# Local attention in a hybrid block: two heads per score matmul, row sums over 128 partitions, queries on the partitions of the result

## The chip, the cores and the metric

The kernel runs on one core of a Trainium2 chip. The metric is the device time of one execution in microseconds. PE is the matmul engine (its weight loads are listed apart, as PEld), DVE the vector engine, ACT the scalar engine, POOL is GpSimd, SP the queue that issues transfers. [...]

## The reference

A windowed-attention block with an MLP, then a landmark attention and a mixture of experts. The change lies in the first of these, which is the only part quoted (x is 16 x 32 x 32 x 128, windows of 8 x 8 tokens, 16 heads of 8 channels):

```python
win = shifted.reshape(B, H_ // WS, WS, W_ // WS, WS, C).transpose(0, 1, 3, 2, 4, 5).reshape(-1, N, C)
qkv = (win @ qkv_w.T + qkv_bias).reshape(-1, N, 3, NH, hd).transpose(2, 0, 3, 1, 4)
attn = jnp.einsum('bhnd,bhmd->bhnm', _l2n(q), _l2n(k)) * scale
attn = attn + rpb[None]                        # relative position bias
attn = attn.reshape(-1, nW, NH, N, N) + ATTN_MASK[None, :, None]
attn = jax.nn.softmax(attn.reshape(-1, NH, N, N), axis=-1)
out = jnp.einsum('bhnm,bhmd->bhnd', attn, v).transpose(0, 2, 1, 3).reshape(-1, N, C)
out = out @ proj_w.T + proj_b
x = x + _ln(out, norm1_g, norm1_b)
```

## The kernel before

The program is a row of phases (setup, this attention, MLP, landmarks, an iterated inverse, mixing, experts) with a barrier between them. Only the attention phase and a few constants of the setup are touched.

The attention phase works on 128 pairs of windows (16 images, 8 pairs each; 128 tokens on 128 partitions). It is written out without loops: `beats` calls each engine's `beat(s)` for s from -5 on, and the order inside `beat` is that engine's order. A beat holds stages of several pairs. In beat s, PE does: `scores` of pair s+1 (L627, 16-bit, only for the row maxima), the projection of pair s-2 (L673, L674), transposes (of q and k, L682, in even beats; of x, L692, in odd ones), `turned_scores` of pair s (L640 brings in maxima and mask, L645 the 32-bit scores, keys on partitions), the transpose of the maxima of s+1 (L704), and `values` of pair s-1 (L662). In odd beats it ends with the q, k products (L716, L717) and the v product (L721) for the two pairs s+5 and s+6. In `values`, both the outputs (`vd`) and the row sums (`den`) are matmuls whose result has channels on partitions, four accumulated parts for each.

DVE does in a beat: reciprocal of the sums of s-2 (L545), normalized output `onT` (L548), row maxima of s+1 (L554), statistics and first half of the layer norm of s-2 (L561 to L566), a slice of the inverse norms of q and k, and the output row (L602). ACT in even beats: squares (L495), `qT` (L501), four masked copies `km` (L504, one head of every four each), exp of pair s (L516), the maxima `mT` of s+1 (L522). In odd beats: `xT` (L512), exp, `mT`, then `qk` (L527) and `vd` (L532) out of PSUM. POOL multiplies the exponentials by the exponential of the position bias (L483) between exp and `values`.

The wait before the transpose of the maxima matters below. Bank 5 of PSUM is shared by it, by the transposes of x and by the v product:

```python
                            if s.odd:
                                unit(pe, xT_ok, s + 5)
                            else:
                                unit(pe, v_ok, s + 4)
```

`met` and `unit` wait for the named signal of a pair or of a unit of two pairs. `apart` adds an instruction between two waits.

## Time and profile before

| what | us |
|---|---|
| median of 3 runs | 4109.78 |
| lowest, highest of them | 4073.84, 5130.18 |
| the profiled execution, its own time | 4067.03 |
| its span in the trace | 4065.2 |
| mean granted TensorE clock over the span | 0.809 |

The span is what the trace shows, and the profiled execution took 1.8 us more than it. All rows come from that one execution. A clock of 1.00 in a view is 2.4 GHz, 0.50 is 1.2 GHz, and a value between is a mean over a stretch that held both. "issue" as a releaser means that the engine waited for nothing that the profile shows.

### The profile page before, as it was taken

Reading aid. Unit: us, or ns where it says so; the run is one execution under the profiler, and the core shown is the slowest. Engines: PE = TensorE matmul, PEld = TensorE weight load, DVE = VectorE, ACT = ScalarE, POOL = GpSimd, SP = SyncE. Lnnn points to the kernel's source line nnn. Section 1 sums busy time; section 2 is a strip of 40 time slices with the busy share of each in tenths; the row PEclk is TensorE's granted clock in tenths of the full one; section 3 lists DMA queues with packets and bytes.
Section 4 is the critical chain, followed back from the end, with each engine's and each line's share of the span. In section 5 each row is a group of like instructions: output and inputs, shape, how many; then the busy total and the mean of one; then the engine's idle time right before and its main releaser. Section 6 shows DMA issues by size and latency. Waiting matters only on the chain. (4 is left out here: it accounts for less than half of the span.)

```text
span 4065.2 us, 136261 instructions
## 1 busy us (share of the span) xinstructions
PE 3284.9 (81%) x55527; PEld 2395.2 (59%) x55527; DVE 2493.4 (61%) x6382; ACT 1486.0 (37%) x2726; POOL 1295.9 (32%) x1363
## 2 busy tenths in 40 slices
PE   3787777777787897999988888888874999877777
PEld 2555555555555575777788665555653666555444
DVE  3555565555565455888777677666663777555555
ACT  1323332233232343333300333333322677545454
POOL 1333333333333232111000155555553000244444
PEclk9756665666666898999989888777776999988888
DMA  2000000000000121000000011111113444322222
GB/s 85 17 17 18 17 18 17 17 17 17 17 18 14 55 71 54 22 21 21 11 4 3 25 49 42 42 40 37 47 34 81 97 96 96 79 63 63 62 63 57
DMA packets 298547, 165.00 MB, mean 41 GB/s; under 512 B 98300, under 2 KB 289160, under 8 KB 297736
## 3 DMA queue, kind: packets, MB, share of 16 engines
q1 hardware_dynamic: 281608, 123.42, 11.3%
q0 software_dynamic: 16384, 33.59, 2.8%
q8 instruction: 420, 6.88, 0.7%
q14 instruction: 135, 1.11, 0.1%
HBM read 67.00 MB, written 71.30 MB: 34 GB/s over the span
## 5 line engine op out<-in xcount | busy, mean ns | idle before, releaser
L2251 DVE TENSOR_TENSOR e_glo<-e_g,e_ghi 128x512 f16<-128x512 f32 x540 | 373.4, 691 | 270.0 <-ACT e_ghi L2158 188.9
L2153 ACT ACTIVATE e_g<-psum,b 128x512 f32<-128x512 f32 x540 | 368.9, 687 | 387.1 <-PE psum L2307 255.6
L2324 PE MATMUL psum<-w2hi,e_ghi 128*128 (+1 forms) x2160 | 419.3, 227 | 99.8 <-DVE e_glo L2251 72.0
L2137 POOL DMA_INDIRECT e_got<-ys_dram,e_idx x256 | 257.8, 1007 | 698.7 <-DMA ys_dram<-e_yo 421.3
L2328 PE MATMUL psum<-w2hi,e_glo 128*128 (+1 forms) x2160 | 415.2, 227 | 10.0 <-issue 9.5
L2326 PE MATMUL psum<-w2lo,e_ghi 128*128 (+1 forms) x2160 | 415.2, 227 | 9.1 <-issue 7.9
L483 POOL TENSOR_TENSOR pT<-pT,rpbx 128x1024 f32<-128x1024 f32 x128 | 301.1, 2352 | 192.8 <-ACT pT L516 192.8
L2324 PEld LDWEIGHTS psum<-w2hi,e_ghi 128*128 128x128 f16 x2160 | 219.1, 101 | 234.6 <-DVE e_glo L2251 112.7
L545 DVE RECIPROCAL rd<-psum 128x128 f32<-128x128 f32 x128 | 122.5, 957 | 300.3 <-PE psum L662 297.6
L1687 POOL DMA_INDIRECT xs_dram<-m_xt,m_idxl x256 | 265.4, 1037 | 113.3 <-issue 72.6
L554 DVE TENSOR_REDUCE mx<-psum 128x16 f16<-128x1024 f32 x128 | 156.2, 1220 | 195.2 <-PE psum L627 194.8
L2326 PEld LDWEIGHTS psum<-w2lo,e_ghi 128*128 128x128 f16 x2160 | 219.6, 102 | 55.9 <-issue 21.6
L2158 ACT ACTIVATE e_ghi<-psum,b 128x512 f16<-128x512 f32 x334 | 227.8, 682 | 0.0
L2328 PEld LDWEIGHTS psum<-w2hi,e_glo 128*128 128x128 f16 x2160 | 220.3, 102 | 10.2 <-issue 9.6
L662 PE MATMUL psum<-pT,den 64*32 64x64 f32 x8192 | 164.4, 282 | 73.6 <-issue 73.6
L662 PE MATMUL psum<-pT,vd 64*32 64x64 f32 x8192 | 159.7, 292 | 78.0 <-issue 76.6
L472 POOL TENSOR_TENSOR rstd<-mv,eps 128x1 f32<-128x1 f32 x128 | 24.2, 189 | 602.7 <-DVE mv L564 602.7
L1973 PEld LDWEIGHTS psum<-m_zd,m_p1T 128*128 128x128 f32 x1024 | 147.6, 222 | 87.6 <-issue 59.7
L1973 PE MATMUL psum<-m_zd,m_p1T 128*128 128x34 f32 x1024 | 154.7, 301 | 40.0 <-issue 25.3
L645 PE MATMUL psum<-qT,km 32*64 32x64 f32 x8192 | 166.1, 304 | 24.0 <-issue 23.9
L662 PEld LDWEIGHTS psum<-pT,den 64*32 64x32 f32 x8192 | 130.3, 130 | 88.1 <-issue 88.1
L1922 PE MATMUL psum<-m_klm,m_qT 128*128 128x512 f32 x256 | 182.2, 804 | 0.0
(331 smaller groups left out, 8010.4 us busy)
## 6 DMA issues: line engine op xcount, KB each, us to landing
ys_dram<-e_yo SPq DMA_DIRECT2D x71, 256.0 KB
f_xm<-x_dram SPq DMA_DIRECT2D x32, 256.0 KB
mid_dram<-f_xm SPq DMA_DIRECT2D x32, 256.0 KB
l_t<-mid_dram SPq DMA_DIRECT2D x16, 512.0 KB
m_t<-mid_dram SPq DMA_DIRECT2D x16, 512.0 KB
res_dram<-m_rest SPq DMA_DIRECT2D x16, 512.0 KB
e_acc<-res_dram SPq DMA_DIRECT2D x32, 256.0 KB
out_dram<-e_acc SPq DMA_DIRECT2D x32, 256.0 KB
```

The lines of the kernel that those rows point to most:

```text
L483: gp.tensor_tensor(pT[:, s.odd], pT[:, s.odd], rpbx[:], ALU.mult).then_inc(pe_ok.sem, 1)
L662: i = pe.matmul(bank(6 + w)[rows(c), N * k:N * k + N], wt, pT[half(w), q.odd, 4 * c + h, :], start=(h == 0), stop=(h == 3), skip_group_che ...
L1687: gp.indirect_dma_start(out=xs, out_offset=bass.IndirectOffsetOnAxis(idxl[w.odd][:, k, t:t + 1], 0), in_=xt16[w.odd][:, t].rearrange("p h ...
L1922: pe.matmul(bank(2 + q.r), qT[q.odd][:, q.t * P:(q.t + 1) * P], klm[q.odd][:].rearrange("p h l -> p (h l)"), start=True, stop=True)\
L1973: i = pe.matmul(bank(6)[:, n * h:n * h + n], p1T[:, j.r, h, :], zd[j.odd][:, h].rearrange("p a d -> p (a d)"), start=True, stop=True)
L2137: gp.indirect_dma_start(out=got[:, q % 2, k, t, :], out_offset=None, in_=ys, in_offset=bass.IndirectOffsetOnAxis(idx[:, q // 2, i:i + 1], 0))\
L2153: ac.activation(g32[:, c % 4, :], bank(c % 4), ACT.Gelu, bias=bias, scale=1.0 / WSCALE)\
L2158: ac.activation(ghi[:, c % 4, :], bank(c % 4), ACT.Gelu, bias=bias, scale=1.0 / WSCALE)\
L2251: ve.tensor_tensor(glo[:, c % 4, :], g32[:, c % 4, :], ghi[:, c % 4, :], ALU.subtract)\
L2324: pe.matmul(o, ghi[:, c % 4, g], w2hi[:, e, f, :], start=first and t == 0, stop=False, skip_group_check=True)
L2326: pe.matmul(o, ghi[:, c % 4, g], w2lo[:, e, f, :], start=False, stop=False, skip_group_check=True)
L2328: i = pe.matmul(o, glo[:, c % 4, g], w2hi[:, e, f, :], start=False, stop=True, skip_group_check=True)
```

## The change

The scores are laid out anew. The masked operand is now q (`qm`, two heads side by side in 128 columns) and not k, so that `scores` has 16 matmuls of 128 result partitions (two heads by 64 queries), and `turned_scores` has 16 + 16 matmuls of 128 columns where there were 32 + 32 of 64. The exponentials of two heads then lie one above the other on 128 partitions. `values` becomes `sums`: 16 matmuls, whose stationary operand is a 128 x 64 block of exponentials and whose moving operand is `vd`, 18 columns wide and block-diagonal: 8 channels and a column of ones for the upper head, 8 and ones for the lower one. Row sums come with the outputs, and queries stand on partitions, so the reciprocal is of 16 numbers per partition (`rs`) and the result `on` must be transposed (a new PE step, a new copy `onT` by ACT) ahead of the projection.

`vd` must hold the tokens of a window twice, so `xT` is written twice over, and the v product runs once per pair (`value_rows`, in every beat) with the window's tokens doubled, copied out by two activations of 64 partitions. The x1 row and its store move one beat later, the layer norm to the end of DVE's beat, and squares on ACT from the even beat's start to the odd beat's end. The phase gets one more beat. In the setup, the bias table is written in two halves, and `den1` is gone.

```diff
...
-                vd = keep("vd", [P, 4, 8, 160])
-                den1 = keep("den1", [P, 4, 32])
...
+                vd = keep("vd", [P, 4, 4, NH // 2, 2, HD + 1])
...
+            qm = sb("qm", [P, 2, 2, 2, 2, 2, N])
             mT = sb("mT", [P, 2, P], F16)
-            pT = sb("pT", [P, 2, NH, N])
...
+            pT = sb("pT", [P, 2, 4, 2, 2 * N])
...
-                            gp.tensor_tensor(pT[:, s.odd], pT[:, s.odd], rpbx[:], ALU.mult).then_inc(pe_ok.sem, 1)
+                            p = pT[:, s.odd]
+                            e = rpbx[:].rearrange("p (j g) n -> p j (g n)", j=4).unsqueeze(2).to_broadcast([P, 4, 2, 2 * N])
+                            gp.tensor_tensor(p, p, e, ALU.mult).then_inc(pe_ok.sem, 1)
...
+                    def value_rows(q):
+                        if q.real():
+                            met(ac, v_ps, q)
+                            met(ac, o_ps, q - 8)
+                            for k in range(2):
+                                half = slice(64 * k, 64 * k + 64)
+                                src = bank(5)[half, 256:512].rearrange("p (w h k d) -> p w h k d", w=2, k=2, d=HD)
+                                i = ac.activation(vd[half, q.u, 2 * q.odd:2 * q.odd + 2, :, k, 0:HD], src[:, :, :, k, :], ACT.Copy)
+                            i.then_inc(v_ok.sem, 1)
+                    def masked(q, g):
+                        if q.real():
+                            ac.activation(qm[:, q.u % 2, :, g % 2, :, g // 2, :],
+                                          bank(4)[:, 0:2 * P].rearrange("p (a w t) -> p a w t", a=2, w=2), ACT.Copy, scale=msk[:, g:g + 1]).then_inc(qm_ok.sem, 1)
                     def beat(s):
                         if not s.odd:
...
                             q = s + 2
                             if q.real():
                                 unit(ac, tr_ps, q)
...
+                                ac.activation(kT[:, q.u % 2].rearrange("p a t -> p (a t)"), bank(4)[:, 2 * P:4 * P], ACT.Copy)\
+                                    .then_inc(kT_ok.sem, 1)
+                            masked(q, 0)
+                            masked(q, 1)
                         else:
                             q = s + 5
                             if q.real():
...
+                                met(ac, v_ps, q - 3)
+                                ac.activation(xT[:, q.u % 2], bank(5)[:, 0:2 * P].rearrange("p (a t) -> p a t", t=N).unsqueeze(2)
+                                              .to_broadcast([P, 4, 2, N]), ACT.Copy).then_inc(xT_ok.sem, 1)
+                        q = s - 2
+                        if q.real():
+                            met(ac, onT_ps, q)
+                            met(ac, pj_ps, q - 2)
+                            ac.activation(onT[:, q.odd, :], bank(6)[:, 0:P], ACT.Copy).then_inc(onT_ok.sem, 1)
+                        if not s.odd:
+                            masked(s + 2, 2)
+                            masked(s + 2, 3)
                         if s.real():
                             met(ac, t_ps, s)
...
+                            ac.activation(pT[:, s.odd].rearrange("p j w n -> p j (w n)"), turned, ACT.Exp).then_inc(pr_ok.sem, 1)
+                        if not s.odd:
+                            value_rows(s + 5)
                         q = s + 1
                         if q.real():
                             met(ac, mT_ps, q)
...
                             ac.activation(mT[:, q.odd, :], bank(5)[:, 0:64].bitcast(F16), ACT.Copy).then_inc(mT_ok.sem, 1)
                         q = s + 5
-                        if s.odd and q.real():
...
-                            unit(ac, v_ps, q)
...
+                        if s.odd:
+                            if q.real():
...
+                            value_rows(q)
+                            if q.real():
...
-                            ve.reciprocal(rd[:], outs[:, :, N:2 * N]).then_inc(rd_ok.sem, 1)
...
+                            ve.reciprocal(rs[:], heads_out[:, :, HD]).then_inc(rs_ok.sem, 1)
+                            met(ve, rs_ok, q)
+                            met(ve, onT_ps, q - 2)
+                            ve.tensor_tensor(on[:, q.odd, :].rearrange("p (h d) -> p h d", d=HD), heads_out[:, :, 0:HD],
+                                             rs[:].unsqueeze(2).to_broadcast([P, NH, HD]), ALU.mult).then_inc(on_ok.sem, 1)
                         q = s + 1
                         if q.real():
                             met(ve, s_ps, q)
                             met(ve, mT_ps, q - 2)
                             ve.tensor_reduce(mx2[:, q.kind(), :].rearrange("p (j r) -> p j r", j=4)[:, :, 0:4],
...
+                        unit(pe, kT_ok, q)
+                        unit(pe, qm_ok, q, 4)
                         met(pe, pr_ok, q - 2)
                         met(pe, mx_ok, q - 1)
-                        apart(pe)
...
+                        for w in range(2):
+                            for k in range(2):
                                 for j in range(4):
...
-                                                  high(qT[rows(j), q.u % 2, q.odd, half(w)]),
...
+                                    i = pe.matmul(bank(j)[:, 64 * (2 * w + k):64 * (2 * w + k) + 64],
+                                                  high(qm[rows(j), q.u % 2, q.odd, k, w].rearrange("p g t -> p (g t)")),
+                                                  high(kT[rows(j), q.u % 2, q.odd, half(w)]), start=True, stop=True)
                         i.then_inc(s_ps.sem, 1)
                     def turned_scores(q):
                         met(pe, mx_ok, q + 1)
                         met(pe, mT_ok, q)
-                        apart(pe)
...
+                        for w in range(2):
+                            for k in range(2):
+                                for j in range(4):
+                                    pe.matmul(bank(j)[half(k), 256 + P * w:256 + P * w + P], selk[rows(j), q.kind(), 2 * w + k, :],
+                                              mT[rows(j), q.odd, :], start=(w == 0), stop=False, skip_group_check=True)
+                        for w in range(2):
+                            for k in range(2):
+                                for j in range(4):
+                                    i = pe.matmul(bank(j)[half(k), 256 + P * w:256 + P * w + P],
+                                                  kT[rows(j), q.u % 2, q.odd, half(w)],
+                                                  qm[rows(j), q.u % 2, q.odd, k, w].rearrange("p g t -> p (g t)"),
+                                                  start=False, stop=(w == 1), skip_group_check=True)
+                        i.then_inc(t_ps.sem, 1)
+                    def sums(q):
+                        met(pe, pe_ok, q)
+                        met(pe, v_ok, q)
+                        met(pe, on_ok, q - 1)
+                        for j in range(4):
+                            for g in range(2):
+                                for w in range(2):
+                                    h = 2 * j + g
+                                    i = pe.matmul(bank(7)[half(w), 2 * (HD + 1) * h:2 * (HD + 1) * (h + 1)],
+                                                  pT[:, q.odd, j, w, N * g:N * g + N],
+                                                  vd[:, q.u, 2 * q.odd + w, h].rearrange("p k d -> p (k d)"), start=True, stop=True)
+                        i.then_inc(o_ps.sem, 1)
+                    def value_rows(q):
+                        if q.real():
+                            unit(pe, xT_ok, q)
+                            met(pe, v_ok, q - 1)
                             for w in range(2):
...
-                    def values(q):
...
-                        apart(pe)
...
-                                        wt = vd[half(w), q.u, 4 * q.odd + c, 32 * h:32 * h + 32] if k == 0 else den1[half(w), h, :]
...
+                                i = pe.matmul(bank(5)[:, 256 + C * w:256 + C * w + C],
+                                              xT[:, q.u % 2, 2 * q.odd + w].rearrange("p r t -> p (r t)"), wqkT[:, 2 * C:3 * C],
+                                              start=True, stop=True)
+                            i.then_inc(v_ps.sem, 1)
...
                         q = s + 5
-                        if s.odd and q.real():
+                        if not s.odd:
+                            met(pe, mT_ok, s)
+                            value_rows(q)
+                        elif q.real():
...
+                            met(pe, v_ok, q - 1)
                             met(pe, mT_ok, s)
                             for a in range(2):
                                 i = pe.transpose(bank(5)[:, P * a:P * a + P], xw[:, q.p + a, :], ident[:])
                             i.then_inc(xT_ps.sem, 1)
+                        q = s - 2
+                        if q.real():
+                            met(pe, on_ok, q)
+                            met(pe, h_ok, q - 1)
+                            pe.transpose(bank(6)[:, 0:P], on[:, q.odd, :], ident[:]).then_inc(onT_ps.sem, 1)
                         if s.real():
                             turned_scores(s)
...
-                                unit(pe, v_ok, s + 4)
+                                met(pe, v_ok, s + 5)
                             pe.transpose(bank(5)[:, 0:64].bitcast(F16), mx2[:, q.kind(), :], ident16[:]).then_inc(mT_ps.sem, 1)
+                        q = s - 2
+                        if q.real():
+                            met(pe, onT_ok, q)
+                            pe.matmul(bank(6)[:, P:2 * P], onT[:, q.odd, :], projT[:], start=True, stop=False)
+                            pe.matmul(bank(6)[:, P:2 * P], ones16[0:64, :], pb2[:], start=False, stop=True)\
+                                .then_inc(pj_ps.sem, 1)
                         q = s - 1
                         if q.real():
-                            values(q)
+                            sums(q)
...
                             met(pe, mT_ok, s + 1)
...
+                            value_rows(q)
...
```

PE in an odd beat before, from `scores` to `values`, and in an odd beat now:

```order
L627 MATMUL psum<-km,qT 64x64 x32
L673 MATMUL psum<-projT,onT 128x128
L674 MATMUL psum<-pb,ones 128x128
L692 MATMUL psum<-ident,xw 128x128 x2
L640 MATMUL psum<-mT,selk 64x64 x32
L645 MATMUL psum<-qT,km 64x64 x32
L704 MATMUL psum<-ident,mx 128x128
L662 MATMUL psum<-pT,vd 32x64 x32
L662 MATMUL psum<-pT,den 32x64 x32
```

```order
L654 MATMUL psum<-kT,qm 128x64 x16
L724 MATMUL psum<-ident,xw 128x128 x2
L730 MATMUL psum<-ident,on 128x128
L666 MATMUL psum<-mT,selk 64x128 x16
L671 MATMUL psum<-qm,kT 64x128 x16
L741 MATMUL psum<-ident,mx 128x128
L745 MATMUL psum<-projT,onT 128x128
L746 MATMUL psum<-pb,ones 128x128
L686 MATMUL psum<-vd,pT 64x18 x16
```

The five groups of 32 become four groups of 16, the projection moves behind the transposed maxima, and the transpose of `on` (L730) is new. ACT in an even beat before, and now (`qm`, `vd`, `onT` as above):

```order
L495 ACTIVATE sq<-qk 128x512
L501 ACTIVATE qT<-psum 128x256
L504 ACTIVATE km<-psum,msk 128x2x128 x4
L516 ACTIVATE pT<-psum 128x1024
L522 ACTIVATE mT<-psum 128x128
```

```order
L519 ACTIVATE kT<-psum 128x256
L510 ACTIVATE qm<-psum,msk 128x2x2x64 x2
L534 ACTIVATE onT<-psum 128x128
L510 ACTIVATE qm<-psum,msk 128x2x2x64 x2
L541 ACTIVATE pT<-psum 128x1024
L504 ACTIVATE vd<-psum 64x16x8 x2
L548 ACTIVATE mT<-psum 128x128
```

The `vd` copies of pair s+5 now stand between exp and `mT`, and in even beats PE's transpose of the maxima (L741) waits for them.

## Rows read from the trace of the kernel before

**Rows 1.** The page: span, and granted clock in 40 equal slices, in tenths.

```profile
span 4065.2 us, 136261 instructions
...
PEclk9756665666666898999989888777776999988888
```

**Rows 2.** Attention phase: length, busy us of PE, PEld, DVE, ACT, POOL; clock, DMA.

```profile
75.00:1340.00 1265.00, 977.80 (x34304) 702.47 (x34302) 700.93 (x1536) 384.36 (x832) 449.41 (x511) 0.65 0.06 17
```

**Rows 3.** Row maxima (L554) by line: count, first and last start.

```profile
L554 DVE TENSOR_REDUCE mx<-psum x128: 1211/1223/1226, 89.4 to 1313.4; 128x16 f16<-128x1024 f32 x128
```

**Rows 4.** Idle of the weight loads by line and releaser: total us, times, longest.

```profile
PEld psum L662 <- issue: 169.6, 117, 2.5
...
PEld psum L673 <- DVE onT L548: 58.5, 50, 1.7
...
PEld psum L627 <- issue: 40.1, 88, 2.3
PEld psum L645 <- issue: 27.3, 19, 2.9
```

**Rows 5.** Weight loads in the setup, in order: start, length, idle before.

```profile
31.34 1.80 PEld L320 LDWEIGHTS psum<-cpw,relx 128*32 128x32 f32 x128 [1.93 <-issue]
```

**Rows 6.** Weight loads in two beats of the attention, in order.

```profile
1009.69 0.89 PEld L645 LDWEIGHTS psum<-qT,km 32*64 32x64 f32 x64
...
1010.81 0.68 PEld L662 LDWEIGHTS psum<-pT,vd 64*32 64x32 f32 x63
...
1014.41 0.16 PEld L662 LDWEIGHTS psum<-pT,den 64*32 64x32 f32 x9 [2.36 <-issue]
...
1023.99 0.40 PEld L662 LDWEIGHTS psum<-pT,den 64*32 64x32 f32 x19 [1.79 <-issue]
...
1027.50 0.93 PEld L721 LDWEIGHTS psum<-wqkT,xT 128*128 128x128 f32 x4 [0.22 <-issue]
...
1031.19 1.20 PEld L645 LDWEIGHTS psum<-qT,km 32*64 32x64 f32 x64
...
1032.72 0.93 PEld L662 LDWEIGHTS psum<-pT,vd 64*32 64x32 f32 x63
...
1035.26 0.51 PEld L662 LDWEIGHTS psum<-pT,den 64*32 64x32 f32 x42 [1.24 <-issue]
```

**Rows 7.** DMA by queue, 1000 to 1100 us.

```profile
q8 instruction: 21, 0.34, 1.6%
```

**Rows 8.** Granted clock in short stretches of the attention and of the inverse.

```profile
1007.20:1017.20 10.00, 6.24 (x305) 4.75 (x305) 8.23 (x13) 4.42 (x11) 3.50 (x4) 0.99 0.05 12
1020.00:1034.00 14.00, 12.45 (x378) 8.86 (x378) 5.73 (x14) 5.67 (x12) 3.56 (x5) 0.50 0.06 17
2087.80:2090.30 2.50, 2.25 (x71) 2.06 (x67) 1.48 (x5) 0.00 (x0) 1.02 (x4) 1.00 0.00 0
2094.30:2096.30 2.00, 1.93 (x36) 1.96 (x38) 1.35 (x4) 0.00 (x0) 0.00 (x0) 0.50 0.00 0
```

**Rows 9.** Weight loads of 64x64 in the iterated inverse, moving operand of 16 columns.

```profile
2088.83 1.36 PEld L1434 LDWEIGHTS psum<-p_ay,p_xs 64*64 64x64 f32 x43 [0.33 <-issue]
```

**Rows 10.** Weight loads of 64x64 there, at the lower clock.

```profile
2094.34 2.88 PEld L1434 LDWEIGHTS psum<-p_t,p_ay 64*64 64x64 f32 x52 [1.16 <-issue]
```

**Rows 11.** Weight loads of 128x128 in the landmark phase.

```profile
1650.91 1.86 PEld L1271 LDWEIGHTS psum<-l_v,l_p3T 128*128 128x128 f32 x16
```

**Rows 12.** Costliest groups by line, 100 to 1300 us.

```profile
L483 POOL TENSOR_TENSOR pT<-pT,rpbx 128x1024 f32<-128x1024 f32 x124 | 291.7, 2353 | 187.7 <-ACT pT L516 187.7
...
L516 ACT ACTIVATE pT<-psum 128x1024 f32<-128x1024 f32 x123 | 127.3, 1035 | 114.0 <-PE psum L645 114.0
...
L545 DVE RECIPROCAL rd<-psum 128x128 f32<-128x128 f32 x123 | 117.7, 957 | 286.1 <-PE psum L662 283.4 <-issue 2.5
...
L522 ACT ACTIVATE mT<-psum 128x128 f16<-128x128 f16 x123 | 35.6, 289 | 0.0
```

**Rows 13.** Who waited for whom, PE, 100 to 1300 us.

```profile
PE psum L640 <- DVE mx L554: 14.0, 37, 0.9
```

More of the change, by code:

```diff
@@ L243, in _ @@
                             n += 1
-                        for k in range(4):
+                        for k in range(2):
                             gp.wait_ge(s_po, n)
-                            gp.memset(den1[:, k, 8 * k:8 * k + 8], 1.0).then_inc(s_po, 1)
+                            gp.memset(vd[64 * k:64 * k + 64, :, :, :, k, HD:HD + 1].rearrange("p u a h d -> p (u a h) d"), 1.0)\
+                                .then_inc(s_po, 1)
                             n += 1
+                        gp.wait_ge(s_po, n)
                         gp.wait_ge(s_ac, 2)
@@ L266, in _ @@
                         ac.wait_ge(s_ac, 4)
-                        ac.activation(rpbx[:].rearrange("q h n -> q n h"), sig[:], ACT.Exp, scale=16.0).then_inc(s_ac, 1)
+                        for k in range(2):
+                            half = slice(64 * k, 64 * k + 64)
+                            ac.activation(rpbx[half].rearrange("q h n -> q n h"),
+                                          sig[half].rearrange("q n (h k) -> q n h k", k=2)[:, :, :, k], ACT.Exp, scale=16.0)\
+                                .then_inc(s_ac, 1)
                     @block.vector
@@ L431, in beats @@
             def beats(eng, body):
-                for s in range(-5, NP * NB + 3):
+                for s in range(-5, NP * NB + 4):
                     body(Pair(0, s))
@@ L452, in beat @@
                         load(s + 8)
-                        q = s - 2
+                        q = s - 3
                         if q.real():
@@ L515, in beat @@
                             met(ac, o_ps, s - 2)
-                            ac.activation(pT[:, s.odd].rearrange("p (j g) n -> p j (g n)", j=4), turned, ACT.Exp)\
-                                .then_inc(pr_ok.sem, 1)
+                            ac.activation(pT[:, s.odd].rearrange("p j w n -> p j (w n)"), turned, ACT.Exp).then_inc(pr_ok.sem, 1)
+                        if not s.odd:
+                            value_rows(s + 5)
                         q = s + 1
@@ L598, in beat @@
                             k = q.p % 4
-                            met(ve, h_ok, q)
-                            met(ve, rstd_ok, q)
-                            met(ve, xb_ok, q)
-                            ve.scalar_tensor_tensor(out=x1[:, q.p, :], in0=h1[:, q.odd, :], scalar=rstd[:, k:k + 1],
-                                                    in1=x1[:, q.p, :], op0=ALU.mult, op1=ALU.add).then_inc(x1_ok.sem, 1)
+                            y = bank(6)[:, P:2 * P]
+                            met(ve, pj_ps, q)
+                            ve.bn_stats(st[:, k, :], y).then_inc(st_ok.sem, 1)
+                            met(ve, st_ok, q)
+                            apart(ve)
+                            ve.bn_aggr(mv[:, k, :], st[:, k, :]).then_inc(mv_ok.sem, 1)
+                            met(ve, mv_ok, q)
+                            ve.scalar_tensor_tensor(out=h1[:, q.odd, :], in0=y, scalar=mv[:, k, 0:1], in1=g1[:],
+                                                    op0=ALU.subtract, op1=ALU.mult).then_inc(h_ok.sem, 1)
                     beats(ve, beat)
@@ L635, in turned_scores @@
                         met(pe, mT_ok, q)
-                        apart(pe)
-                        for g in range(4):
-                            for w in range(2):
-                                for j in range(4):
-                                    pe.matmul(bank(j)[half(w), 256 + 64 * g:320 + 64 * g], selk[rows(j), q.kind(), g, half(w)],
-                                              mT[rows(j), q.odd, half(w)], start=(g == 0), stop=False, skip_group_check=True)
-                        for g in range(4):
-                            for w in range(2):
-                                for j in range(4):
-                                    i = pe.matmul(bank(j)[half(w), 256 + 64 * g:320 + 64 * g],
-                                                  km[rows(j), q.u % 2, q.odd, g, half(w)], qT[rows(j), q.u % 2, q.odd, half(w)],
-                                                  start=False, stop=(g == 3), skip_group_check=True)
@@ new lines, in turned_scores @@
+                        for w in range(2):
+                            for k in range(2):
+                                for j in range(4):
[3 more added lines that the diff above has]
+                                                  start=False, stop=(w == 1), skip_group_check=True)
@@ L719, in beat @@
                             met(pe, mT_ok, s + 1)
-                            for a in range(2):
-                                i = pe.matmul(bank(5)[:, 2 * P + C * a:2 * P + C * a + C], xT[:, q.u % 2, P * a:P * a + P],
-                                              wqkT[:, 2 * C:3 * C], start=True, stop=True)
-                            i.then_inc(v_ps.sem, 1)
+                            value_rows(q)
                     beats(pe, beat)
```

133 lines of the change are left out of this document (43 added, 90 removed).

## The prediction

> **What bounds the kernel now.** I read the slices of the page first, then the attention phase alone, then who waits for whom in it, and last its instructions in order of time. The change touches one phase only, from about 75 to 1340 us of a span of 4065.2 us [rows 1, 2]. In it PE is busy 978 of 1265 us, DVE 701, ACT 384 and POOL 449, and the granted clock is 0.65, which mixes 1.2 GHz for about 70% of the time with 2.4 GHz for about 30% [rows 2]. The row maxima come 128 times with first starts 1224 us apart [rows 3], so a beat takes 1224 / 127 = 9.64 us, and each us saved per beat is worth 128 us, each us per two beats 64.
>
> PE's stream is what sets the beat, and the reader should look at its idle time. Between 100 and 1300 us (124.5 beats) the weight loads of `values`, `scores` and the 32-bit scores wait 169.6 + 40.1 + 27.3 = 237 us for nothing that the profile shows [rows 4], which is 1.90 us per beat. In order of time these are holes of 1.2 to 2.4 us in the middle of a group, with no operand missing: 2.36 us ahead of the last 9 loads of `values`, 1.79 ahead of the last 19, 1.24 ahead of the last 42 [rows 6]. The setup shows the pattern bare: 128 loads (256 instructions with their matmuls) take 1.80 us, and then 1.93 us are lost [rows 5], a period of 3.73 us for 256 instructions. In the attention 21 packets of kind instruction arrive in 100 us, 0.34 MB in all, so 16 KB each, one per 256 instructions of 64 bytes [rows 7]. My reading: PE outruns the supply of its own code wherever it gets through 256 instructions in less than 3.7 us. `values` (256 instructions) with the scores before it (128) does so in every beat; from the refill at 1023.99 to the hole at 1035.26 stand about 512 instructions and no hole between [rows 6], since q, k and v products are slow ones. The rest of PE's idle time is DVE's: 58.5 us for `onT` [rows 4] and 14.0 for the maxima [rows 13], 0.58 us per beat.
>
> **The change part by part**, at an unchanged clock, summed over 128 beats against the profiled execution (4067.03 us, 1.8 above its span; the median of the runs, 4109.78, lies 1% above it, and the lowest run at 4073.84 beside it).
>
> 1. Supply holes. Per beat PE had 256 small passes and about 15 others, so some 545 instructions or 2.1 refills per beat. Now `scores` has 16 passes, `turned_scores` 16 + 32, `sums` 32, and with the rest it is about 111 passes, 225 instructions, 0.9 refills in a beat of 8 us or more. Nowhere do 256 instructions fit into 3.7 us. The holes go: -1.90 x 128 = -244 us.
>
> 2. `values` to `sums`. Without holes 63 passes of `values` take 0.93 us at the low clock and 0.68 at the high one [rows 6], so 128 passes some 1.7 and 1.3 us, 1.6 at today's mixture. A pass of `sums` loads a 128 x 64 32-bit block for 18 columns, and the trace has no such pass. Nearest is the inverse: 64x64 blocks for 16 columns, alternating between two places of the array as `sums` does, 43 loads in 1.36 us, so 29 ns at the clock 1.00 [rows 8, 9], and 52 loads in 2.88 us, so 52 ns, at 0.50 with wider operands [rows 8, 10]. 32 passes are then 0.93 or 1.66 us, 1.45 mixed: -0.15 x 128 = -19 us. The bounds: below, the setup's 14 ns per 32-column load [rows 5], 0.45 us, another -128; above, one load after the other by the 112 ns of 128 columns [rows 11], halved to 56 ns, or 1.8 us at the high clock and 3.6 at the low one, 3.0 mixed, +198. I take the inverse, which has the same width and the same two places.
>
> 3. Score matmuls. The 32-bit ones stream the same columns in half the passes (64 loads took 0.89 to 1.20 us [rows 6]); I take -0.08 us, -10; between 0 and half of their time, -70. `scores` loads 128 columns 16 times where it loaded 64 columns 32 times, but only four places of the array run side by side, not eight: +0.2 us, +26, between 0 and +64.
>
> 4. The v product runs per pair on doubled tokens: 4 passes per beat where there were 4 per two beats. They took 1.15 us at the low clock (from 1027.50 to 1028.65, where the next load stands), about 0.65 at the high one: +1.0 per two beats, +64. The transpose of `on` is one more full-width pass, 0.3 us with its fill: +38.
>
> 5. A new wait. In even beats the transpose of the maxima (L741) now waits for the `vd` copies of pair s+5, which stand on ACT behind exp(s). Exp needs the end of `turned_scores`, the group right ahead of L741 on PE. So PE stands still for exp, 1.03 us [rows 12], two copies of 128 numbers per partition, 0.5 to 0.6 going by the `mT` copy at 289 ns [rows 12], and 0.1 to 0.2 of signals: 1.7 us per two beats, +109. Queued behind it on PE are the projection, `sums` and the next scores. The bounds: 1.3 if ACT starts early, and 2.5 if it is late, because ahead of exp it also has `onT` and four masked copies (1.56 us in the old even beat).
>
> 6. DVE. The reciprocal shrinks from 957 ns [rows 12] to that of 16 numbers; I take 0.2 us. PE's 0.58 us per beat of waiting for DVE falls to about 0.3: in even beats transposes and v product cover DVE's maxima (1.22 us [rows 3]), in odd ones reciprocal, `on` and maxima (1.8 us) outlast scores and transposes by some 0.6. So -0.29 x 128 = -37. POOL's multiplication, 2.35 us [rows 12], starts up to 2 us later, behind the layer norm's two steps, and has most of a beat; it costs nothing while the beat is above some 5.5 us. The later x1 row and squares are covered in the same way. One more beat at the end, mostly drain: +6. The setup's edits hide behind its transfers: 0.
>
> Sum: -244 - 19 - 10 + 26 + 64 + 38 + 109 - 37 + 6 = -67 us.
>
> 7. The clock. Here the trace shows 0.99 in the 10 us from 1007.2 and 0.50 in the 14 us from 1020 [rows 8]; the fall comes after the 2.36 us hole and the waits behind it, and the slices stay at 0.6 wherever there are such holes, against 0.9 and more in phases whose PE is unbroken [rows 1]. With the holes gone there is one gap of 1.7 us and one of 0.6 in two beats, where there were about five. I take the share of 2.4 GHz from 0.3 to 0.47. The work of PE, some 15 us in two beats, takes about a third less at 2.4 GHz (0.89 against 1.20 us, 0.68 against 0.93 [rows 6], 29 against 52 ns [rows 9, 10]), so a tenth of share is worth 0.55 us per two beats, 35 us: -60. The ends: all of it lost, +105; a share of 0.8, -175.
>
> **Forecast:** 4067 - 67 - 60 = 3940 us.
>
> [...]
>
> **The rivals.**
>
> A, serial weight loads, the other side. If the two column halves don't load side by side, a pass costs its load and its 18 columns: 56 + 15 ns at the high clock, 112 + 30 at the low one, 120 mixed, 3.9 us per beat in place of 1.45. That is +310 us: 4067 - 67 + 310 = 4310 us, and with less of the rest filled perhaps 4250. It decides from (1.45 + 127 / 128) / 32 = 76 ns per pass. For it: 112 ns per 128-column load [rows 11]. Against it: 29 ns in the inverse, and the 14 ns of the setup. [...]
>
> B, holes that stay. If a hole comes at each refill whatever the pace, 0.9 of 2.1 remain, +105: 4067 - 67 + 105 = 4105 without the clock's gain; if they have another cause and all remain, 4244. Against it: the 512 instructions without a hole. [...]
>
> C, no gain in clock. Fewer columns stream per beat than before, and if PE's gaps hold it at 1.2 GHz, item 7 gives 0 to +60: 4000 to 4060, little or no change.
>
> D, an unbroken PE. A clock share of 0.7 or more, or `sums` near the setup's pace: 4067 - 67 - 175 = 3825, down to 3760.
>
> **How the numbers follow.** Chances: forecast 0.50 (its own range 3870 to 3995), C 0.19, D 0.18, A 0.08, B 0.05. A measurement of this kernel tells some 2% (80 us) from no change. Faster by over 2% is below some 3990: nearly all of the forecast's, D, a fifth of C: 0.70. Slower by over 2%: A and a third of B, 0.10. The rest, 0.20. The range leaves out A, B's upper part and D's lower end, 3800 to 4075.
>
> **What the changed profile would show.** Rows of `sums`, scores and their loads without "issue" holes of over a us; beats of 8.6 us by the maxima's starts; L741 waiting some 1.7 us 64 times on ACT's `vd` copies; 32 passes of L686 in 1 to 1.7 us; a clock in the phase around 0.73. Wrong would be: holes in L686 or L671, L686 above 2.4 us, a clock below 0.6, or PE waiting for ACT's `onT` ahead of the projection.

## The result, and the profile after

The changed kernel takes 3950.43 us (median of 4 runs, 3931.93 to 3964.55). Against the undisturbed runs of the kernel before (4109.78 and 4073.84; two more, above 5000, were disturbed and are left out) the ratio is 0.9652, 95% interval 0.954 to 0.9763. The profiled execution took 3962.64, its span is 3960.9, so 104 us less than the 4067.03 that the sum was made against.

The page of the changed kernel, span and granted clock in 40 slices:

```profile
span 3960.9 us, 96572 instructions
...
PEclk9666566665658989999898767777758999888888
```

Some 40,000 instructions fewer, and a clock that in the first eleven slices is no better than in [rows 1].

The attention phase and, behind it, mixing and experts (busy us of PE, PEld, DVE, ACT, POOL; clock; DMA):

```profile
68.00:1185.00 1117.00, 947.76 (x14205) 680.29 (x14205) 624.34 (x1532) 481.78 (x1151) 442.67 (x510) 0.62 0.06 17
```
```profile
2120.00:2930.00 810.00, 674.04 (x3328) 493.52 (x3327) 535.18 (x1688) 256.14 (x531) 409.18 (x351) 0.73 0.12 38
2990.00:3945.00 955.00, 811.35 (x8013) 539.07 (x8011) 581.33 (x1097) 553.68 (x869) 257.27 (x256) 0.91 0.30 74
```

Between the barriers, which stand in the trace as PE's drains, the attention takes 1117.8 us where it took 1268.6, so it gained 151. The mixing phase takes 839.4 (before 811.6) and the experts 983.4 (before 965.9) with the same instructions; the other phases agree within 2 us. That is 45 us given back by phases that the change doesn't touch, and the reason why only 104 of the 151 are seen in these two executions. Mixing ran at a lower clock (0.73 against 0.77); why, and why the experts were slower, no run shows. In run 5 below they are not.

The row maxima by line:

```profile
L582 DVE TENSOR_REDUCE mx<-psum x128: 1211/1219/1225, 93.3 to 1169.0; 128x16 f16<-128x1024 f32 x128
its engine sat idle before it (us, times) until:
  PE psum L654: 239.2, 64
who waited for it (us, times):
  PEld psum L666: 61.5, 65
  PE psum L666: 42.0, 65
```

A beat is (1169.0 - 93.3) / 127 = 8.47 us, against 9.64 from [rows 3].

Who waits for whom on PE, 100 to 1250 us (total, times, longest):

```profile
PE psum L741 <- ACT vd L504: 110.3, 62, 2.1
PE psum L666 <- DVE mx L582: 42.0, 65, 0.8
...
PE psum L730 <- DVE on L576: 2.9, 5, 0.7
```

The waits for nothing of [rows 4] (237 us in the weight loads of `values` and scores) have no successor: L686 and L671 are not among the waits for "issue" any more, and L654 has 61 of some 0.2 us, 13.7 us in all. In their place stands one wait, 1.78 us in every even beat.

Two beats of the changed kernel in order of time (start, length, idle before):

```profile
700.98 1.02 ACT L541 ACTIVATE pT<-psum 128x1024 f32<-128x1024 f32 x1
701.90 0.56 ACT L504 ACTIVATE vd<-psum 64x128 f32<-64x128 f32 x2
...
702.61 0.22 PE L741 MATMUL psum<-ident,mx 128*128 128x128 f16 x1 [1.77 <-ACT vd L504]
...
703.18 1.29 PEld L686 LDWEIGHTS psum<-vd,pT 128*64 128x64 f32 x32
...
704.63 0.26 DVE L573 RECIPROCAL rs<-psum 128x16 f32<-128x16 f32 x1 [0.24 <-PE psum L686]
...
706.40 0.20 PEld L666 LDWEIGHTS psum<-mT,selk 32*64 32x64 f16 x16 [0.95 <-DVE mx L582]
...
708.59 1.79 PEld L686 LDWEIGHTS psum<-vd,pT 128*64 128x64 f32 x32
```

The reader sees PE stand still through exp and the two `vd` copies, then 32 passes of `sums` without a hole: 1.79 us in the odd beat (56 ns a pass), 1.29 in this even one. Over 45 pairs of beats, counted to the next group's first load, the two values are 1.83 and 1.33, and the odd beat lasts 10.00 us with hardly any spread (9.99 to 10.01), the even one 7.19.

### The profile page after: what moved, and what is told of

The parts are those of the page before. It is cut to its first block and busy times, and to the rows that moved or that the text cites. A ratio compares the mean times of both kernels' runs of the same rounds, so it can differ in the third digit from the quotient of the medians.

```text
span 3960.9 us, 96572 instructions
## 1 busy us (share of the span) xinstructions
PE 3296.6 (83%) x35431; PEld 2399.9 (61%) x35431; DVE 2417.4 (61%) x6382; ACT 1583.9 (40%) x3047; POOL 1287.3 (33%) x1360
## 5 line engine op out<-in xcount | busy, mean ns | idle before, releaser
L490 POOL TENSOR_TENSOR pT<-pT,rpbx 128x1024 f32<-128x1024 f32 x128 | 300.2, 2345 | 20.9 <-ACT pT L541 20.9
L686 PE MATMUL psum<-vd,pT 128*64 128x18 f32 x4096 | 210.2, 254 | 0.0
L2013 PEld LDWEIGHTS psum<-m_zd,m_p1T 128*128 128x128 f32 x1024 | 156.9, 234 | 87.3 <-issue 58.4
L686 PEld LDWEIGHTS psum<-vd,pT 128*64 128x64 f32 x4096 | 196.1, 195 | 12.1 <-POOL pT L490 0.2
L2013 PE MATMUL psum<-m_zd,m_p1T 128*128 128x34 f32 x1024 | 163.2, 312 | 38.2 <-issue 24.2
L1962 PE MATMUL psum<-m_klm,m_qT 128*128 128x512 f32 x256 | 193.1, 849 | 0.0
L541 ACT ACTIVATE pT<-psum 128x1024 f32<-128x1024 f32 x128 | 131.3, 1026 | 108.7 <-PE psum L671 107.7
L1743 ACT ACTIVATE m_p1T<-psum 128x512 f32<-128x512 f32 x128 | 76.4, 597 | 230.2 <-PE psum L1954 127.2
L759 PE MATMUL psum<-wqkT,xT 128*128 128x256 f32 x256 | 156.1, 712 | 1.4 <-ACT xT L528 1.4
```

Source lines behind the costliest of these rows:

```text
L490: gp.tensor_tensor(p, p, e, ALU.mult).then_inc(pe_ok.sem, 1)
L686: i = pe.matmul(bank(7)[half(w), 2 * (HD + 1) * h:2 * (HD + 1) * (h + 1)], pT[:, q.odd, j, w, N * g:N * g + N], vd[:, q.u, 2 * q.odd + w, ...
L1962: pe.matmul(bank(2 + q.r), qT[q.odd][:, q.t * P:(q.t + 1) * P], klm[q.odd][:].rearrange("p h l -> p (h l)"), start=True, stop=True)\
L2013: i = pe.matmul(bank(6)[:, n * h:n * h + n], p1T[:, j.r, h, :], zd[j.odd][:, h].rearrange("p a d -> p (a d)"), start=True, stop=True)
```

## The experiments

They ran in two later jobs, on chips with the numbers 4 (runs 1 to 4) and 1 (runs 5 to 8), where the experts take 766 to 769 us for every kernel, not 966; the first comparison's chip has no number on record, and I take it for another one. So the kernel before takes 3800.57 (runs 1 to 4) and 3831.73 (runs 5 to 8) there, and what is compared is the ratio on the same chip and the attention phase, whose length hardly depends on the chip: run 5, the changed kernel again, shows it (1118.5 us against 1117.8). The kernel before has no trace from those two chips, so its 1268.6 us are from the first. The absolute times in the expectations of runs 1 and 4 are meant for the first chip.

**Run 5, the changed kernel again.** No edit.

> The changed kernel as it is, on the chip of this job, so that the other runs have it beside them. Expected: attention phase 1115 to 1120 with a granted clock near 0.6 in 75:1270, a beat of 8.47, and about 150 less than the kernel before in that phase, so a ratio near 0.96. If the chip itself made the 150, the ratio would be nearer 0.98 here.

Measured: 3670.72, ratio 0.9596 (0.9559 to 0.9632), attention 1118.5 (1117.8 on the first chip), clock in it 0.61. The gain of 151 us in the phase is the change's own. The mixing phase took 761.0 here and the experts 768.0, so the 45 us that they gave back in the first comparison are not.

**Run 1, the `vd` copies early.**

```diff
                             masked(q, 0)
                             masked(q, 1)
+                            value_rows(s + 5)
...
-                        if not s.odd:
-                            value_rows(s + 5)
```

> The changed kernel, complete and with the reference's result, with one move: on ACT, in even beats, the two copies of pair s+5 into vd stand right behind the first two masked copies, no longer behind exp(s). PE's transpose of the maxima (L741) then finds them done. In the changed kernel PE waits there 110.3 us in all. If that wait is a real loss on the path, the beats shrink from 8.47 us to about 7.6 and the attention phase by 95 to 110 us, since exp starts half a us later but its reader has room: the time is about 3850. If the clock also depends on PE's gaps, the granted clock of the phase rises above 0.63 and some 50 us more go: 3800. Rival: the wait is only where another one shows, the maxima or the multiplication on POOL take its place, and the time stays above 3930.

**Run 6, the same kernel** beside run 5.

> The changed kernel with ScalarE's copy of the v rows (value_rows of pair s+5) issued right behind the masked copy in the even beats. Theory (the wait of L741 for the vd copies keeps both the 110 of wait and a part of the clock): attention phase 965, 150 under the changed kernel, ratio 0.925 to the kernel before. Rival (the first chip was just cooler): under 110 gained and a clock that stays at 0.6.

Measured: 3510.10, ratio 0.9249 (0.9219 to 0.928), and 3522.90, ratio 0.9206 (0.9183 to 0.9228); attention 965.1 and 965.6. That is 153 us less than the changed kernel, for one line moved, and more than the whole of the wait (110.3 us). Waits on PE of run 6, 100 to 1200 us, its line numbers one lower:

```profile
PE psum L665 <- DVE mx L581: 50.4, 65, 1.0
PE psum L685 <- POOL pT L490: 40.3, 48, 2.6
...
PE psum L740 <- ACT vd L504: 12.8, 26, 0.6
```

The attention phase of run 6, and of run 5 beside it:

```profile
68.00:1032.00 964.00, 824.83 (x14205) 586.53 (x14205) 663.52 (x1532) 474.20 (x1151) 447.96 (x510) 0.73 0.07 20
```
```profile
68.00:1185.00 1117.00, 948.12 (x14205) 680.31 (x14205) 624.68 (x1532) 481.60 (x1151) 442.61 (x510) 0.61 0.06 17
```

The same 14205 matmul passes keep PE busy for 825 us instead of 948. The wait on ACT fell by 98 us, a new one on POOL's multiplication took 40, that on the maxima 8 more; the clock's rise from 0.61 to 0.73 moves the share of the higher level of the clock (1.00) from 0.22 to 0.46, at the prediction's 35 us per tenth another 84. Sum -133, measured -153. In time order (run 1):

```profile
607.24 0.57 ACT L504 ACTIVATE vd<-psum 64x128 f32<-64x128 f32 x2
...
607.96 0.22 PE L740 MATMUL psum<-ident,mx 128*128 128x128 f16 x1 [0.62 <-ACT vd L504]
...
608.72 1.03 ACT L542 ACTIVATE pT<-psum 128x1024 f32<-128x1024 f32 x1
608.74 1.01 PEld L685 LDWEIGHTS psum<-vd,pT 128*64 128x64 f32 x32
```

**Run 4, work in the gap.** Is it the gap that keeps the clock down? Nine 16-bit matmuls of 224 columns, whose result nobody reads, ahead of the wait in even beats.

```diff
+                            if not s.odd:
+                                for n in range(9):
+                                    pe.matmul(bank(7)[:, 288:512], ident16[:], w1hi[:, 0, 0:224], start=True, stop=True)
```

> The changed kernel with nine 16-bit matmuls of 224 columns into unused PSUM in every even beat, behind the turned scores, where PE otherwise waits some 1.8 us for the copies into vd. They take 0.85 us at 2.4 GHz and 1.7 at 1.2. If gaps in PE's stream hold the granted clock at 0.63, it rises with the gap filled, to 0.8 or more in the phase, and the time falls by 50 to 150 us although PE has more to do. If the clock doesn't depend on this gap, it stays near 0.63, and the time stays within 10 us of the changed kernel's or grows by up to 40 us.

Measured: 3578.57, ratio 0.9418 (0.9397 to 0.9439), attention 1014.1. With more work and no wait removed from the path, the phase is 104 us shorter. The time fell as expected; the clock rose to 0.77 and not to the 0.8 that was named. Its window and PE's longest wait, 100 to 1050 us:

```profile
68.00:1082.00 1014.00, 871.89 (x14782) 628.21 (x14783) 655.33 (x1532) 477.15 (x1152) 443.25 (x510) 0.77 0.07 19
```
```profile
PE psum L744 <- ACT vd L504: 64.3, 62, 1.4
```

Of the gap of 1.78 us, 1.04 is left (64.3 / 62), and the filler takes about 1.0 (1.04 us in most beats). So PE is held up slightly longer than before, by 0.27 us in an even beat, 17 in all. The clock is what changed: 0.62 to 0.77, a share of 0.24 to 0.54, at 35 per tenth -105. Sum -88, measured -104. So PE's stop in the even beat kept the clock down. The filler also gives PE more to do, which could be a cause of its own; against that speak run 6, where the clock rises to 0.73 with the same 14205 passes once the stop is gone, and run 3 below, where 144 more passes a beat with the stop left in place (112.1 us in L741) go with a clock of 0.58.

**Run 2, the kernel before with fewer sums.** 48 of the 128 passes of `values` left out: of the row sums of four heads per quarter only the first is computed, into all four places, so the divisor is wrong for the others.

```diff
-                            gp.memset(den1[:, k, 8 * k:8 * k + 8], 1.0).then_inc(s_po, 1)
+                            gp.memset(den1[:, k, 8 * k:8 * k + 8] if k else den1[:, 0, :], 1.0).then_inc(s_po, 1)
...
-                            for h in range(4):
+                            for h in range(4 if k == 0 else 1):
...
-                                                      start=(h == 0), stop=(h == 3), skip_group_check=True)
+                                                      start=(h == 0), stop=(h == 3 or k == 1), skip_group_check=True)
```

> The kernel before with fewer passes in its row sums: of the 64 den passes of a beat only 16 are left, with a full block of ones, so all four heads of a group get the sum of the first one (the output is not the reference's). DVE's work is the same. 48 passes are 96 instructions less per beat, 449 in place of 545, and 0.6 us of PE work. If the holes are the supply of code, PE saves the work and more than half a us of holes per beat: beats of 8.3 to 8.5 us against 9.64, about 150 us less. If the holes have another cause and stay at 1.9 us per beat, only the work goes and some of it turns into waiting: 30 to 75 us less.

Measured: 3655.23, ratio 0.962 (0.9599 to 0.9641), attention 1113.5, so 155 below the 1268.6 of the kernel before, in beats of 8.43 us. The same gain as the whole change, from leaving out 48 passes a beat. Its waits on PE, 100 to 1150 us:

```profile
PE psum L673 <- DVE onT L548: 88.4, 58, 3.3
PE psum L662 <- issue: 72.4, 68, 2.2
PE psum L627 <- issue: 18.5, 34, 1.7
PE psum L645 <- issue: 14.8, 10, 2.8
```

The 48 passes themselves cost 10.8 to 14.8 ns each by [rows 6] (0.68 and 0.93 us for 63), 13.6 mixed: 0.65 us a beat, 83 in all. The rest came from the holes. I cut PE's instructions into blocks of 256 (counted from the first hole on) and took the largest gap at each block's end, over some 124 beats of each kernel (100 to 1300 us before, 100 to 1150 here and in the changed kernel): 246 us in the kernel before, 133 here, 16 in the changed kernel. 83 + 113, less some 36 that PE now waits longer for `onT` (88.4 against 52.3 in those beats), is 160; the clock, 0.63 against 0.65, would take back some 14 of it. Had the holes stayed as they were, the gain would be at most the 83; the run shows 155.

Where the holes stand says the most. Number everything that the trace records of PE (loads, matmuls, and its register and semaphore instructions) in order of start, and look at the idle times of 1 us or more before a weight load that have no releaser. In the kernel before, 100 to 1300 us, there are 122, and 121 of them stand at the same place of every 256 instructions (at one of two neighbouring remainders). Since a beat isn't a multiple of 256 instructions, that place wanders through the code: 95 fall in L662, 12 in L627, 12 in L645, 2 in L716. In this run it is 65 of 66 (within four places), in run 8 138 of 139; the changed kernel has none, apart from the loads ahead of L741, whose matmul waits for ACT. No wait for an operand and no property of one group would keep to such a count. The transfers keep to it: from 100 to 1100 us the queue of kind instruction moved 218 packets of 16 KB in the kernel before and 104 in the changed one, while the trace records 55787 and 26888 instructions of PE. That is one packet per 256 and 259 of them, 2.1 and 0.9 a beat.

**Run 3, more instructions in the changed kernel.** 144 tiny matmuls (32 x 32 weights, one column) in each beat ahead of `sums`.

```diff
+                            for n in range(144):
+                                c = n % 4
+                                pe.matmul(bank(7)[rows(c), 300:301], ident16[rows(c), 0:32], ones16[rows(c), 0:1],
+                                          start=True, stop=True)
```

> The changed kernel with 144 tiny 16-bit matmuls (32x32 weights, one column, into unused PSUM) ahead of sums in each beat, so that PE has about 513 instructions per beat, near the 545 of the kernel before. The array work is some 0.6 to 0.9 us per beat, and nothing waits for it. Code supply: holes of 1 to 2.5 us with no operand missing come back in the tiny matmuls or in sums, about 1.1 us per beat in all, and beats go to about 10.3 us. Rival, in which the holes came from the old values matmuls themselves (their 64x32 tiles, their order of tiles, their operands): no hole, beats of 9.2 to 9.4 us.

Measured: 3974.88, ratio 1.0461 (1.0439 to 1.0483), attention 1423.9, a beat of 10.84. The costliest groups of weight loads, 100 to 1400 us:

```profile
L686 PEld LDWEIGHTS psum<-vd,pT 128*64 128x64 f32 x3744 | 214.6, 224 | 27.7 <-issue 25.8
L752 PEld LDWEIGHTS psum<-ones,ident 32*32 32x32 f16 x16971 | 176.0, 95 | 56.9 <-issue 32.5
```

Holes are back in groups that had none. Of 1 us or more there are 23 (those ahead of L741 again left out), 12 in the filler and 11 in `sums`, and all 23 stand at the same place of every 256 instructions, which rules out the rival, that the old `values` matmuls made them. Cut into blocks as in run 2, by the time that a block's 256 instructions took without the gap at its end (number of blocks, mean gap):

| | under 2 us | 2 to 2.7 | 2.7 to 3.3 | 3.3 to 4 | over 4 |
|---|---|---|---|---|---|
| before | 38, 1.92 | 80, 1.32 | 16, 1.53 | 40, 0.66 | 87, 0.19 |
| run 2 | 6, 2.04 | 64, 1.18 | 12, 0.82 | 19, 0.59 | 114, 0.21 |
| changed | 0 | 0 | 0 | 0 | 109, 0.15 |
| run 3 | 28, 1.24 | 15, 0.86 | 37, 0.43 | 13, 0.28 | 145, 0.07 |

A gap follows where PE was fast, and the faster the longer; the changed kernel has no block under 4 us at all. Where the gap is over 1 us, a block with its gap has a median of 3.84 us before and of 3.3 in run 3. The gaps of run 3 are 77 us, smaller than I expected (0.5 us a beat and not 1.1), since three blocks in five took over 4 us. The sum is 8.47 + 1.65 for the filler's own loads + 0.5 = 10.6; the clock's fall from 0.62 to 0.58 makes most of the rest. These blocks are my cut, not a view of the profile, and what else may fill a gap at a block's end (a wait of another kind) is in them.

**Run 8, only the reciprocal shortened, in the kernel before.** Beyond the first pair it works on 8 of 64 columns per window, and the others keep old values.

```diff
-                            ve.reciprocal(rd[:], outs[:, :, N:2 * N]).then_inc(rd_ok.sem, 1)
+                            n = N if q.b == 0 and q.p == 0 else 8
+                            ve.reciprocal(rd[:, :, 0:n], outs[:, :, N:N + n]).then_inc(rd_ok.sem, 1)
```

> The kernel before, with the reciprocal of 8 of each 64 columns per window (128x16 numbers in place of 128x128), as many as the changed kernel has; the rest of the columns keep the first pair's, so that the output is not the reference's. It asks what the shorter VectorE work alone gives. Theory (the time came from fewer TensorE instructions): the attention phase gains at most 20. Rival (VectorE's chain was what the beat followed): 60 or more.

Measured: 3818.60, ratio 0.9982 (0.996 to 1.0004), so no change clear of noise; attention 1264.4, 4 less than before. The waits say where the time went, 100 to 1200 us:

```profile
PE psum L663 <- issue: 140.0, 106, 2.4
PE psum L646 <- issue: 29.7, 26, 2.2
PE psum L628 <- issue: 23.7, 16, 2.4
PE psum L674 <- DVE onT L549: 17.2, 43, 0.5
```

The wait for `onT`, 46.4 us in the kernel before over the same stretch, fell to 17.2. But the holes filled the room: 193 us in `values` and both score groups, against 181 before (135.2 + 23.9 + 21.4). PE ran into the next hole the earlier. DVE's shorter work alone gave nothing here, where the holes were the limit.

**Run 7, POOL's multiplication first.** On top of run 6, POOL does L490 (now L476) ahead of the norm's two steps and the x1 row.

```diff
                     def beat(s):
+                        if s.real():
+                            met(gp, pr_ok, s)
+                            p = pT[:, s.odd]
...
                         q = s - 2
```

> The vd copies early, and GpSimd does the multiplication of the probabilities (L490) ahead of the two others of its beat. In the kernel with the early copies the sums wait 43 for it (49 times, 3.1 longest) and their weight loads 51. Theory: that wait goes, 40 less, ratio 0.914. Rival: the operations of the residual and the norm that now come later on GpSimd make VectorE and so the scores wait as long: ratio 0.925, no gain.

Measured: 3513.31, ratio 0.9182 (0.9157 to 0.9207), attention 963.7, 1.9 less than run 6. The wait on POOL went, as both theories had it, and hardly any time with it; what came was neither's, a transfer (37.7 us against 3.8 in run 6):

```profile
PE psum L665 <- DVE mx L581: 48.9, 65, 0.8
PE psum L723 <- DMA xw<-in_x: 37.7, 22, 3.4
PE psum L710 <- DVE qk L617: 11.1, 17, 0.7
```

The x rows' buffers are freed by POOL's x1 row, which now runs last in its beat and waits longer for the store of the old x1 (171.3 us against 97.6 in run 6, 100 to 1000 us). That the late refill comes from there is argued from the program and these rows, not tested.

## Why the prediction was right and where it failed

The forecast of 3940 us lies within 0.3% of the median, and its sign and range are right. Against the profiled execution (3962.64) three errors nearly cancel: the clock was 81 us worse than forecast, the sum at an unchanged clock 105 us better, and phases that the change doesn't touch gave back 45. That the number came so near is luck.

**Item 7, the clock, is the step that failed.** It took the share of the higher level from 0.3 to 0.47 (-60 us), because five gaps in two beats would become two. Measured, the clock in the phase went from 0.65 to 0.62, a share of 0.24, which at the item's own 35 us per tenth is +21. The prediction had both gaps in its hands (1.7 and 0.6 us) and counted them, where one of them decided: runs 4, 1 and 6 show that the single stop of 1.8 us per even beat holds the clock down, since it rises to 0.73 or more when that stop is filled or taken away. Whether it does so by its length or by its place no run separates. Even then the share is 0.46 to 0.54: with this stop gone, item 7 would have been about right. Rival C had the clock's side right, that PE's gaps hold it down; its time of 4000 to 4060 did not come, since the sum at an unchanged clock was off.

**The same-clock sum, -67, was mis-sized.** The phase gained 151 in spite of the clock, so about -172 at an unchanged clock. The groups of PE's stream, from one group's first weight load to the next one's, mean of 45 pairs of beats in us per two beats; the waits are taken out by the waits' totals, and the groups of the kernel before are those without a hole (of `values` only 4 of 90 groups are, so its 3.36 is an estimate from few). Each column is at its own kernel's clock:

| | before | after | x 64 | forecast |
|---|---|---|---|---|
| holes | 3.80 | 0 | -243 | -244 |
| waits for DVE | 1.16 | 0.71 | -29 | -37 |
| wait for `vd` | 0 | 1.78 | +114 | +109 |
| `values`, `sums` | 3.36 | 3.16 | -13 | -19 |
| `scores` | 0.70 | 0.63 | -4 | +26 |
| 32-bit scores and selection | 2.84 | 2.26 | -37 | -10 |
| q, k, v products | 3.64 | 4.94 | +83 | +64 |
| all transposes, that of `on` too | 2.13 | 2.15 | +1 | +38 |
| projection | 1.62 | 1.56 | -4 | 0 |
| not assigned | 0.23 | 0 | -15 | |
| sum | 19.48 | 17.19 | -147 | -73 |

(The forecast's extra beat, +6, is not in the table.) The three terms that carry the argument, holes, new wait and `sums`, came within 10 us each. What was off are the small ones: halving the number of passes was worth more in the scores than I gave it (that `scores` would lose 0.2 us a beat by four places of the array in place of eight was my estimate, and no run shows it), and transposes and selection, which I left at their old price, got cheaper and paid for the transpose of `on`. Why the transposes got cheaper no run tests.

By item:

- Item 1 right, and its cause is tested from both sides. Leaving out instructions in the old kernel (run 2) gave 155 us, 83 of them the passes' own; adding instructions to the new one (run 3) brought holes back; and the holes keep to one place of every 256 instructions. Rival B is out: with 0.9 refills a beat, 16 us of gaps are left, not 105.
- Item 2 right: 1.33 and 1.83 us for 32 passes, 1.58 in the mean, where 1.45 was taken. Rival A is out: 42 and 57 ns a pass where it needed 76. For one load after the other rival A estimated 71 ns at the high clock, 56 for the load and 15 for its columns, the 15 from no row; run 1's rows have 32 (1.01 us for 32 passes, the fastest seen).
- Item 3 (with the selection, which it left unpriced) too dear by 57 us, item 4 about right for the v product (v alone 0.85 and 1.15 us), its rest in the table.
- Item 5 right in size (1.78 us, 62 times in 1150 us) and cause. Its cost was understated all the same, since it is also the cause of item 7's failure: moved away, the wait is worth 153 us, not 109.
- Item 6 right within 8 us. Run 8 adds that the shorter reciprocal alone is worth some 4, which its interval doesn't tell from nothing: DVE's gain counts only once the holes are gone.
- What the profile was to show came but for one: beats of 8.47 (8.6 forecast), L741 waiting 1.78 (1.7), no holes above a us but the wait itself, and L686 in 1.3 to 1.8 us, but a clock of 0.62 and not 0.73. A clock "below 0.6" was the sign of error, and it stands just above.

The change's best version here is the one of run 6 (or 7): ratio 0.92 to the kernel before, with `vd` copied ahead of exp.

## What to carry to other kernels

Where PE runs through many small matmuls, count its instructions against time before counting columns: here, where a long gap stood, a block of 256 of them with its gap took 3.3 to 3.8 us in the median, and fewer, larger passes gained about what their holes had cost. Price a new wait on PE twice, for its length and for the clock that it keeps down (here 110 us of waiting, and 153 gained when it went and the clock rose from 0.61 to 0.73), and look first at what the program of the engine waited for could do earlier: here one moved line doubled the change's gain. A wait that is removed shows the next one (40 us on POOL in run 6, 38 on a transfer in run 7), so change the order one engine at a time and read the waits again.

## What the runs showed of the hardware

The granted clock has two levels in the traces, 1.00 and 0.50. Three 16-bit passes of 512 columns in a row (L2305 to L2307 of the kernel before) start 216 ns apart at 1.00 and 427 at 0.50, so 2.4 and 1.2 columns a ns; the prediction's 2.4 and 1.2 GHz stand for these two levels.

The clock repeated with the beats. In the changed kernel all 45 odd beats looked at last 9.99 to 10.01 us at a granted clock of 0.50, the lower level (0.53 in the highest; 56 ns a pass of `sums`). The even beats had 0.73 in the mean, and their share of the higher level fell in part into PE's stop (1.00 from 700.9 to 702.6 us, where PE does nothing). With the stop gone (run 6) the same odd beats last between 6.55 and 13.06 us, at clocks from 0.50 to 1.00.

DVE was held up by POOL. The output row, a 128x128 operation with two operands from SBUF, took a mean of 1117 ns in run 6, where it falls beside POOL's multiplication, and 385 ns in run 7, where it never does. Within run 6, the 50 of 126 that don't touch the multiplication took 342 ns, and the 69 that start while it runs took 1658 ns in the mean and ended 0.15 us after it (median). Groups by form, 100 to 1030 us:

```profile
L589 DVE SCALAR_TENSOR_TENSOR x<-h,rstd,x 128x128 f32<-128x128 f32 x126 | 140.8, 1117 | 0.0
```
```profile
L589 DVE SCALAR_TENSOR_TENSOR x<-h,rstd,x 128x128 f32<-128x128 f32 x127 | 48.9, 385 | 69.0 <-POOL rstd L484 68.9
```

In run 7 this line's 92 us less were not all saved: two other operations got slower (L617 took 938 ns against 725 in run 6, L611 659 against 298), and DVE's busy time fell by 62 us (663.5 to 601.6). They bought nothing, since DVE had room.
